# Attention output by token tiles, LN2 statistics in seven operations, part of x + attention on GpSimd, first FFN tiles in blocks of 128

## The reference

```python
x = x + attn(layernorm(x), Wq, Wk, Wv)
x = x + ffn(layernorm(x), W_r, W_k, W_v, mu_r, mu_k)

def attn(x, Wq, Wk, Wv):            # one head of D = 64
    q, k, v = x @ Wq, x @ Wk, x @ Wv
    att = softmax(einsum('bid,bkd->bik', q, k), axis=1)   # over the queries i
    return tile(att @ v, (1, 1, 16))                      # 64 columns, 16 times

def ffn(x, W_r, W_k, W_v, mu_r, mu_k):
    x_prev = x shifted by one token (zeros first)
    xr = mu_r * x + (1 - mu_r) * x_prev
    xk = mu_k * x + (1 - mu_k) * x_prev
    r = sigmoid(xr @ W_r.T)
    return r * (square(relu(xk @ W_k.T)) @ W_v.T)
```

## Time and profile before

| | |
|---|---|
| median of three runs | 393.59 us (393.56 to 395.23) |
| profiled execution | 392.12 us, its span 390.6 us (core 5; cores 386.8 to 390.6) |
| TensorE busy | 313.1 us, 80% |
| ScalarE busy | 229.5 us, 59% |
| VectorE busy | 217.9 us, 56% |
| GpSimd busy | 109.0 us, 28% |
| chain that ended last | PE 48%, ACT 20%, issue 14%, DVE 10%, DMA 4%, POOL 2% |

### The profile page before, as it was taken

How to read it: one execution, slowest core, us unless ns; L and a number is a source line. 1 busy time by engine, 2 the same in 40 slices (tenths; PEclk the granted TensorE clock), 3 DMA queues, 4 the chain that set the end, 5 groups by cost and what they waited for, 6 DMA issues and landing times.

```text
span 390.6 us, 5546 instructions; the slowest of 8 cores (386.8 to 390.6 us)
## 1 busy us (share of the span) xinstructions
PE 313.1 (80%) x1578; PEld 127.5 (33%) x1578; DVE 217.9 (56%) x445; ACT 229.5 (59%) x358; POOL 109.0 (28%) x158
## 2 busy tenths in 40 slices
PE   0467986696869866777536998999999999999993
PEld 0333341231222211111114443444444444444441
DVE  3787889246235321121259987789277918780055
ACT  1442389989799999999849339104840285024500
POOL 2887448608400026888800021001000000000000
PEclk9998897876698986555555899999999999999998
DMA  7999369896899999920000004131423122220014
GB/s 207 297 323 295 109 149 200 165 265 121 117 181 164 178 188 332 343 90 0 1 1 2 0 3 86 28 157 53 79 32 148 68 54 55 107 107 2 0 55 163
DMA packets 40399, 48.10 MB, mean 123 GB/s; under 512 B 31152, under 2 KB 31536, under 8 KB 39984
## 3 DMA queue, kind: packets, MB, share of 16 engines
q1 hardware_dynamic: 39504, 40.98, 37.7%
q0 software_dynamic: 864, 6.75, 10.6%
HBM read 38.74 MB, written 8.39 MB: 121 GB/s over the span
## 4 chain that ended last, share of the span: by engine, by line
PE 48%; ACT 20%; issue 14%; DVE 10%; DMA 4%; POOL 2%; DVEq 0%; ACTq 0%; SPq 0%; POOLq 0%
PE F L1045 13%; PE F L1005 11%; PE F L1023 11%; PE tf L797 5%; ACT junk L1115 5%; ACT junkL L1115 4%; PE F L856 4%; ACT Prot L1115 4%; DMA xst<-x_in 4%; ACT P L1115 3%; DVE xr L646 2%; PE acc L868 2%; ACT z L1143 2%; DVE dxk L655 1%; DVE bnst L458 1%
## 5 line engine op out<-in xcount | busy, mean ns | idle before, releaser
L856 PE MATMUL F<-qk 64*128 64x512 bf16 x136 | 62.0, 476 | 32.1 <-ACT Prot L1115 9.1
L1164 ACT ACTIVATE rr<-F 128x1024 bf16<-128x1024 f32 x16 | 16.4, 1023 | 72.9 <-PE F L1005 72.9
L1005 PE MATMUL F<-wr,xr 128*128 128x512 bf16 x256 | 58.4, 388 | 0.0
L860 PE MATMUL F<-qk 64*128 64x512 bf16 x120 | 57.6, 498 | 0.0
L1045 PE MATMUL F<-wv,ka 128*128 128x512 bf16 x256 | 56.1, 379 | 1.9 <-ACT ka L1172 1.9
L1023 PE MATMUL F<-dxk,wk 128*128 128x512 bf16 x256 | 55.9, 379 | 0.0
L1115 ACT ACTIVATE P<-F,negm 128x1024 bf16<-128x1024 f32 (+1 forms) x40 | 37.2, 947 | 18.5 <-PE F L856 16.3
L1115 ACT ACTIVATE junk<-F,negm 128x1024 bf16<-128x1024 f32 x32 | 39.9, 1260 | 3.0 <-PE F L856 1.7
L856 PEld LDWEIGHTS F<-qk 64*128 64x128 bf16 x136 | 12.5, 97 | 84.1 <-issue 83.0
L1115 ACT ACTIVATE junkL<-F,negm 128x1024 bf16<-128x1024 f32 x32 | 39.9, 1282 | 0.0
L1115 ACT ACTIVATE Prot<-F,negm 128x1024 bf16<-128x1024 f32 x32 | 39.0, 1354 | 0.0
(11 more groups left out here) (105 smaller groups left out, 426.0 us busy)
## 6 DMA issues: line engine op xcount, KB each, us to landing
xst<-x_in SPq DMA_DIRECT2D x32, 512.0 KB, 7.3
x<-x_in SPq DMA_DIRECT2D x16, 512.0 KB, 28.6
y_out<-x SPq DMA_DIRECT2D x15, 512.0 KB, 2.8
wr<-wr_in POOLq DMA_DIRECT2D x1, 2048.0 KB, 15.1
wk<-wk_in POOLq DMA_DIRECT2D x1, 2048.0 KB, 29.3
wv<-wv_in POOLq DMA_DIRECT2D x1, 2048.0 KB, 42.6
y_out<-x SPq DMA_DIRECT2D x2, 256.0 KB, 2.9
wqk<-wqk_in POOLq DMA_DIRECT2D x1, 256.0 KB, 9.3
```

Of the source, the lines that this page charges most:

```text
L856: t.matmul(f[:, 0:512], qk2[0:64, kt * 128:(kt + 1) * 128], qk1[0:64, i0:i0 + 512], start=True, stop=True, skip_group_check=True, tile_pos ...
L860: t.matmul(f[:, 512:1024], qk1[64:128, kt * 128:(kt + 1) * 128], qk2[64:128, i0 + 512:i0 + 1024], start=True, stop=True, skip_group_check= ...
L1005: ins = t.matmul(f[:, hh * 512:(hh + 1) * 512], xr[:, ct, j * 128:(j + 1) * 128], wr[:, ct, hh * 512:(hh + 1) * 512], start=(ct == 0), sto ...
```

## The change

- `out_mm(kt)` has the exponentials of 128 tokens as weights and vs (64 columns) as the moving operand: 16 products of 64 columns, in the order of `LN2OUT`, into acc laid out by token tile. The output is by token at once; the copies of acc, the fp32 transposes and their semaphores are gone. ScalarE copies acc to out_tok in three pieces: tiles 3 to 7, 0 to 2, 8 to 15. The table load for the root stands before the wait for the products.
- out_mm stands behind every second unit only, tiles from 16 on first (`out_after`): 0 to 8 behind units 68 to 84, 16 to 19 to unit 92, then 9 (94), 20 (96), 10 (98) and so on, 15 at unit 118, 29 at 132, 30 and 31 last. x tiles are loaded when theirs is done.
- The loads of wk and wv2 stand behind the folds of tiles 4 and 8.
- `ln2_stats` has seven operations; the first group waits for eight folds only, and comes before any x + attention on VectorE.
- GpSimd adds the attention output to the x tiles of positions 1, 3 and 4 of LN2SEQ (tiles 4, 6, 7), from the first A_TOK on. VectorE adds to positions 0 and 2 behind the group's statistics.
- TensorE turns three z tiles (positions 1, 0, 2), the first two into other PSUM banks, and VectorE evacuates these two. Positions 3 and 4 go by DMA transposes.
- Block 0 is mixed in four blocks of 128 tokens, not two of 128 and one of 256. R(0, 0) and the first half of K(0, 0) wait for each column tile by itself.
- The halo's products stand right behind the last out_mm; its copy before the first x + attention; its two small operations (hx) behind mix_k(0), before the second group's statistics.

```diff
+LN2OUT = [3, 4, 5, 6, 7, 0, 1, 2] + list(range(8, 16))
...
+    for u in range(NB, NU):
+        ready = [k for k in range(KT) if k not in out_pos and last_unit[k] + 4 <= u]
+        if ready and (u - NB) % 2 == 0:
+            kt = min([k for k in ready if k >= 16], default=ready[0])
+            out_after[u] = kt
+            out_pos[kt] = len(out_pos)
...
             def out_mm(kt):
                 t.wait_ge(V_VS, 3 * kt + 3)
-                for w in (0, 2, 1, 3):
-                    half = w // 2
-                    t.matmul(acc[64 * half:64 * half + 64, (w % 2) * 512:(w % 2 + 1) * 512],
-                             vs[:, kt * D:(kt + 1) * D],
-                             own_p(kt)[:, w * 512:(w + 1) * 512],
-                             start=(kt == 0), stop=(kt == KT - 1), skip_group_check=True,
-                             tile_position=(0, 64 * half)).then_inc(P_O, 1)
+                for i, t_ in enumerate(LN2OUT):
+                    ins = t.matmul(acc[:, t_, :], own_p(kt)[:, t_ * 128:(t_ + 1) * 128],
+                                   vs[:, kt * D:(kt + 1) * D],
+                                   start=(kt == out_seq[0] and i % 8 == 0), stop=(kt == KT - 1),
+                                   skip_group_check=True)
+                    if i == 15 or kt == KT - 1 and i == 7:
+                        ins.then_inc(P_O, 1)
...
+            g.wait_ge(A_TOK, 1)
+            for s in GX1:
+                t_ = LN2SEQ[s]
+                g.wait_ge(G_XF, 4 * t_ + 4)
+                g.tensor_tensor(
+                    x1[:, t_, :], x1[:, t_, :],
+                    bass.AP(out_tok, t_ * D, [[TOWN * D, 128], [0, 16], [1, D]]),
+                    ALU.add).then_inc(G_X1, 1)
...
                 v.reduce_sum(so[:, a:b], o, axis=AX.X).then_inc(V_ST2, 1)
...
+                v.scalar_tensor_tensor(w, xf[:, a:b, :], 0.125, o,
                                        ALU.mult, ALU.add).then_inc(V_ST2, 1)
                 v.wait_ge(V_ST2, n + 1)
+                v.scalar_tensor_tensor(od, bass.AP(so, a, [[TOWN, 128], [1, b - a], [0, D]]),
+                                       -1.0 / D, o, ALU.mult, ALU.add).then_inc(V_ST2, 1)
                 v.wait_ge(V_ST2, n + 3)
+                v.tensor_tensor(w, w, od, ALU.mult).then_inc(V_ST2, 1)
                 v.wait_ge(V_ST2, n + 4)
                 v.reduce_sum(sp[:, a:b], w, axis=AX.X).then_inc(V_ST2, 1)
                 v.wait_ge(V_ST2, n + 5)
+                v.scalar_tensor_tensor(vpe2[:, a:b], sp[:, a:b], 1.0 / D, vpe[:, a:b],
                                        ALU.mult, ALU.add).then_inc(V_ST2, 1)
+                v.scalar_tensor_tensor(nmean2[:, a:b], so[:, a:b], -1.0 / D, ag[:, a:b, 0],
+                                       ALU.mult, ALU.subtract).then_inc(V_ST2, 1)
...
             v.wait_ge(A_TOK, 1)
-            ln2_x1(0)
-            v.wait_ge(A_TOK, 2)
-            v.wait_ge(G_XF, 4 * TOWN)
+            v.wait_ge(G_XF, 4 * 8)
             ln2_stats(0)
             ln2_shift(0)
-            for s in range(1, 5):
-                ln2_x1(s)
-            v.wait_ge(D_C, 64)
-            v.wait_ge(A_T2, 2)
+            v.wait_ge(P_H, 2)
+            v.tensor_copy(hs[:, 7:8], F[0][:, 0:1]).then_inc(V_H, 1)
+            ln2_x1(0)
+            ln2_x1(2)
+            v.wait_ge(P_T2, 1)
+            v.tensor_copy(z1T[:, :, c_blk(0):c_blk(0) + 128], tx[1][:, :, :]).then_inc(V_T2, 1)
+            v.wait_ge(P_T2, 2)
+            v.tensor_copy(z1T[:, :, c_blk(0) - 1:c_blk(0)],
+                          tx[0][:, :, 127:128]).then_inc(V_T2, 1)
...
-            mix_d(c_blk(0) + 256, 256, 256, 0, 3)
-            mix_r(c_blk(0) + 256, 256, 256, 0)
+            v.wait_ge(D_T2[1], t2_n(3))
+            mix_d(c_blk(0) + 256, 128, 256, 0, 3)
+            mix_r(c_blk(0) + 256, 128, 256, 0)
+            v.wait_ge(D_T2[0], t2_n(4))
+            mix_d(c_blk(0) + 384, 128, 384, 0, 4)
+            mix_r(c_blk(0) + 384, 128, 384, 0)
```

More of the change, by code:

```diff
@@ L104, in build_program @@
     f_prev = [max([p for p in range(u) if f_of[p] == f_of[u]], default=-1) for u in range(NU)]
+    out_after = {}
+    out_pos = {}
+    for u in range(NB, NU):
[4 more added lines that the diff above has]
+            out_pos[kt] = len(out_pos)
+    for kt in range(KT):
+        if kt not in out_pos:
+            out_pos[kt] = len(out_pos)
+    out_seq = sorted(out_pos, key=out_pos.get)
     ctx = ExitStack()
@@ L300, in build_program @@
         x1_n = lambda q, j: 2 + 4 * q + j
-        NP2 = 5
+        NP2 = 3
+        GX1 = {1: 1, 3: 2, 4: 3}
+        vx1_n = lambda s: s + 1 - sum(p < s for p in GX1)
         t2_n = lambda s: 16 * ((s - NP2) // 2 + 1)
@@ L340, in _ @@
             for t_ in range(TOWN):
-                sy.wait_ge(P_O, 4 * (t_ + 1))
+                sy.wait_ge(P_O, out_pos[t_] + 1)
                 sy.dma_start(out=x1[:, t_, :],
                              in_=x_in[t_ * 128:(t_ + 1) * 128, :]).then_inc(D_R[t_], 16)
+            for s in range(NP2, 5):
+                c0 = 16 + 128 * (LN2SEQ[s] % 8)
+                sy.wait_ge(A_Z1, s + 1)
+                sy.dma_start_transpose(out=z1T[:, :, c0:c0 + 128],
+                                       in_=z1[:, s % 2, :]).then_inc(D_T2[s % 2], 16)
             for q in range(4):
@@ L698, in _ @@
                 if q == 0:
+                    v.wait_ge(V_H, 1)
+                    v.tensor_scalar(hx[:, 0:8], xh[:, :], hs[:, 7:8], None,
+                                    ALU.add).then_inc(V_H, 1)
+                    v.wait_ge(V_H, 2)
+                    v.tensor_tensor(hx[:, 8:16], hx[:, 0:8], hx[:, 0:8],
+                                    ALU.mult).then_inc(V_H, 1)
+                    v.wait_ge(A_TOK, 3)
+                    v.wait_ge(G_XF, 4 * TOWN)
                     ln2_stats(1)
@@ L956, in _, with T2 @@
             VT(3)
-            nxt = begun
-            done = 0
+            assert begun == NB
             t.wait_ge(V_MX, 8)
             t.wait_ge(V_VT, 4)
[L962 to L967, removed]
-            for kt in range(done, KT):
+            for u_ in range(NB, NU):
+                fill(u_)
+                if u_ in out_after:
+                    out_mm(out_after[u_])
+            for kt in out_seq[len(out_after):]:
                 out_mm(kt)
             t.wait_ge(A_EXP, NU)
-            t.wait_ge(D_C, 64)
-            for j in range(8):
-                if j == 0:
-                    t.wait_ge(A_OT, 1)
-                if j == 4:
-                    t.wait_ge(V_OT, 1)
-                ins = t.transpose(F[0][:, j * 128:(j + 1) * 128],
-                                  outT[:, j * 128:(j + 1) * 128], identf[:, :])
-                if j % 4 == 3:
-                    ins.then_inc(P_OTT, 1)
-            def T2(s):
-                if s >= 2:
-                    t.wait_ge(A_T2, s - 1)
-                t.wait_ge(A_Z1, s + 1)
+            for kt in range(KT):
+                for h in range(2):
+                    ins = t.matmul(F[0][64 * h:64 * h + 64, 0:1],
+                                   vs[:, kt * D:(kt + 1) * D],
+                                   junkL[:, halo_unit[kt] % 3, 1054 - kt:1055 - kt],
+                                   start=(kt == 0), stop=(kt == KT - 1),
+                                   skip_group_check=True,
+                                   tile_position=(0, 64 * h))
+                    if kt == KT - 1:
+                        ins.then_inc(P_H, 1)
+            def T2(s, n, to):
+                t.wait_ge(A_Z1, n)
                 for ct in range(CT):
@@ L1003, in R @@
                 for ct in range(CT):
+                    if q == 0 and j == 0:
+                        t.wait_ge(V_XR, ct + 1)
                     for hh in range(2):
@@ L1051, in V @@
                         ins.then_inc(P_F, 1)
-            for s in range(NP2):
-                T2(s)
+            T2(1, 1, tx[1])
+            T2(0, 2, tx[0])
+            t.wait_ge(A_TOK, 3)
+            T2(2, 3, tb[0])
             R(0, 0)
```

159 lines of the change are left out of this document (57 added, 102 removed).

## The result

The changed kernel takes 396.78 us (median of four runs, 396.37 to 396.89) against 393.62 of the kernel before (393.56 to 395.23): ratio 1.0069, 95% interval 1.0042 to 1.0095. It is slower by 3.2 us (0.7%); 395.3 was predicted, from 389.2 to 398.0. Measured again on another chip, beside the experiments, it was 396.78 against 393.88, ratio 1.0073 (1.0052 to 1.0095).

What follows compares the result with a forecast made beforehand. Bound: a serial chain of about 50 us between ScalarE-bound attention and gapless TensorE. Terms -4.20 +5.83 -0.75 +1.15 +0.53 +0.21 -1.11 = +1.66 on 393.59 gave 395.3 us; range 389.2 to 398.0.

Steps and rivals of the forecast that it cites:

- Held adds: LN2 statistics of group 0: GpSimd's three adds and VectorE's two-input operations hold each other for whole instructions, +5.83 us.
- the walk: Statistics to square root, step by step: GpSimd adds alternating with w, od and product, 8.63 us against 2.80.
- The first rival: GpSimd's adds and VectorE's statistics run side by side, nothing held: -4.15, 389.4 us; chance 0.20.
- brief holding: Rival at the statistics: GpSimd's adds hold VectorE, but take near 1.2 us instead of 2.35: 391.8 us; chance 0.13.
- The clock's fall: Rival at V(0, 0): TensorE's clock falls after a gap of about 4 us, +1.9, 397.2; 4 in 10 within each case.
- The likeliest case: Whole kernel: held adds without a fall of the clock, 395.3 us, itself 394 to 396.5; chance 0.37.
- V(0, 0) piece: First V product to R(1, 0): halo products moved to where TensorE waits, -1.11 us; +0.8 if the clock falls.
- Products of 64 columns: Attention output by token tiles: 16 products of 64 columns, 55 ns each at 1.2 GHz, hidden, cost 0.
- The slow end of the range: Attention: products too slow at 1.2 GHz, exponentials starve for units 94 to 118: +3, 398 us; chance 0.05.
- The end of attention: Last vs to LN2 statistics: folding ends near 180, vs takes 0.24, fp32 transposes and copies gone: -4.20 us.
- Statistics no shorter: LN2 statistics of group 0: fewer instructions but no shorter path to the square root, 2.82 against 2.80 us: 0.
- blocks of 128: Mix of block 0: four blocks of 128 take 11.68 us against 10.53: +1.15.

Runs made afterwards that it cites:

- e1: Changed kernel with GpSimd's three x + attention adds given to VectorE, behind the statistics: 394.02 us, ratio 0.9998 to the kernel before.
- e3: Changed kernel with only position 1 added by GpSimd, positions 3 and 4 by VectorE: 394.57 us, ratio 1.0035 to the kernel before.
- e4: Changed kernel with GpSimd filling tiles 4, 6 and 7 with a constant, their adds left out: 391.79 us, ratio 0.9965 to the kernel before.
- e6: Changed kernel with GpSimd's three adds started only after the statistics (after nmr2): 394.64 us, ratio 1.0057 to the kernel before.
- e5: Changed kernel with 12 unused products of 512 columns filling the gap before the first V product: 394.42 us, ratio 1.0026 to the kernel before.
- e7: Changed kernel, GpSimd's adds kept, block 0's last 256 tokens mixed in one block, hx operations moved back, z of position 4 earlier: 393.24 us, ratio 1.0002.
- e8: e2 with the 12 filling products of e5 before the first V product: 390.10 us, ratio 0.9917 to the kernel before.
- e2: e1 with e7's three edits: 392.28 us, ratio 0.9949 to the kernel before.

## Why the prediction came out as it did

**Held adds, the forecast's mechanism: shown.** It was argued from a GpSimd power behind a VectorE add and from a one-input operation of VectorE; e1, e3 and e4 show the missing case, a two-input operation behind a GpSimd add. The term was +5.83 and is +5.63. w took 1.97 where about 2.3 was written, GpSimd's add 2.36 where 2.35 was; the handing to and fro was the walk's: w, add 2, od, add 3, product, their ends 2.55 us apart. The row that the walk rested on, four VectorE adds in 4.63 us around the power, didn't show it, as no add was late there; the second add of e6 does (4.50 for two). The rule in the Trainium skill ("SBUF — State Buffer", Who interferes with whom), that a VectorE instruction with two SBUF inputs contends with a GpSimd one that reads SBUF and not with one that only writes, agrees with this case in both halves: 1.97, 2.62 and 2.44 us beside adds, 0.48 beside a memset (e4). The first rival, 389.4, and brief holding fall.

**The clock's fall: in the rivals with 4 in 10, and it happened.** The likeliest case had left it out, and this is why 395.3 was too low; the same case with the fall was 397.2, and 396.8 was measured. The step of the sum that was mis-sized is the V(0, 0) piece: -1.11 written, +0.36 measured, 1.47 of it the clock (15.57 less the 14.10 that 15.21 - 1.11 gives). The price set, 1.9, was a little high: e5 puts it at 1.6. The gap was forecast at 4 us, and is 2.85: K's products after mix_k ran at 0.55 of the clock from 229.4 to 233, and the gap covered this slowness. Just before, the pieces of K(0, 0) had come one by one, 0.67 us apart with 0.29 idle, each when mix_k had its column tile. That alone isn't the reason for this first fall, though: e6 has the same pauses, its clock stays at 1.00 there, and its gap is 3.75. What else it takes is open, and so is the forecast's rule that the gap's length decides, as e7 shows. The changed kernel, then e6:

```profile
225.00:229.40 4.40, 2.65 (x8) 0.57 (x7) 4.40 (x8) 1.02 (x1) 0.00 (x0) 0.98 0.00 0
229.40:233.00 3.60, 3.57 (x10) 1.31 (x11) 3.28 (x7) 0.00 (x0) 0.00 (x0) 0.55 0.00 0
```
```profile
223.40:227.80 4.40, 2.77 (x11) 0.72 (x9) 4.38 (x8) 1.02 (x1) 0.00 (x0) 1.00 0.00 0
227.80:231.40 3.60, 3.60 (x17) 1.65 (x18) 3.30 (x6) 0.00 (x0) 0.00 (x0) 1.00 0.02 5
```

**Products of 64 columns: right.** 16 take 1.01 us at 1.2 GHz, the last of them 0.24, so 51 ns apart; the other out_mm at this clock have 53 (55 written). First out_mm to last vs is unchanged. The slow end of the range and the rule of the Trainium skill ("TensorE: Matmul & The Clock Gate", Part 3) that a load overlaps only a product of other row groups would have shown as starved exponentials; the measurement decides against them. The clock kept higher for longer in attention, as argued (0.77 in 150 to 165, 0.50 before the change), and was worth nothing there.

**The end of attention: right to 0.2 us, one reason wrong.** The last vs takes 0.24 and statistics start 2.04 behind it. But folding did not end near 180. x tile 9 was asked for at 148.86 and landed at 167.86; the nine tiles before it had taken 3.2 to 5.4 us each. While it was under way, wk (140.12 to 158.29) and wv2 (from 153.47) were loading and the DMA engines were busy throughout (share 1.03 from 154 to 168). So the weights probably stood in its way, against what the forecast says of them, but no run moved them. Core 0's last fold ended at 192.86, 3.7 us before the vs: the 0.24 had less room than was written.

```profile
153.47 0.57 POOL L454 DMA_DIRECT2D wv<-wv_in  x1
...
168.01 1.25 POOL L439 TENSOR_TENSOR fold<-x 128x512 f32<-128x512 f32 x1 [13.97 <-DMA x<-x_in]
```
```profile
154.00:168.00 14.00, 10.87 (x125) 5.90 (x126) 1.69 (x9) 14.00 (x28) 0.04 (x1) 0.75 1.03 196
```

**Statistics no shorter, blocks of 128, hx, statistics 1, halo: right.** The statistics of group 0 took 2.83 us in e1 against 2.80 before and 2.82 written; blocks and hx 1.81 against 1.68; statistics 1 0.16 against 0.21. The halo's -1.11 is seen where the clock is kept: 13.95 from V(0, 0) to R(1, 0) in e5 against 15.21, -1.26. R(0, 0) began 1.3 us after the first mix and gave nothing.

**Not in the sum.** R(1, 0) to the end is 0.78 shorter. TensorE's part is the same in both (110.50 us from R(1, 0) to V(3, 0)), so it lies in the tail behind it: from the end of VectorE's last add to the end of the span, where the last store runs, it is 3.5 us before and 2.65 after in the mean of the cores. And the time rose 0.7 us more than the pieces (3.16 against 2.47), which may be due to the core that happened to be late before the first out_mm. Both were seen, not tested, and the forecast had neither. They nearly cancel, so that 397.2 for the case with the fall comes within 0.4 us of the time is in part luck; the agreement piece by piece is not.

## What to carry to other kernels

Before giving GpSimd a share of VectorE's work, count the SBUF inputs of what VectorE does meanwhile: an operation with two on VectorE and one of GpSimd that reads (here adds, folds and powers) take turns, whole instruction by whole instruction, and a long GpSimd add in front of a chain of short VectorE steps charges every step. Here an add of 1.14 us on VectorE was cheaper than one of 2.35 on GpSimd beside it. When a serial chain ahead of a dense product stream grows, look at TensorE's gap too: its clock can turn a covered wait into a cost behind it, here 1.6 us.

## What the runs showed of the hardware

- Holding works both ways and is handed over at every instruction, also between two that follow each other on one engine: three GpSimd adds alternated with three VectorE operations (7.43 us for what takes 7.1 alone). It applies to fp32 and bf16 alike (the mix of e6, 2.08 against 0.70) and not to a reduction with one input (0.49) or a GpSimd memset (three in 2.73 us). One input doesn't always exempt VectorE: the bf16 scaling of vs took 1.05 and 0.68 us beside GpSimd folds, and 0.24 without.
- A gap of 2.85 us before V(0, 0) let the granted clock fall from 1.00 to 0.50 (2.73 to 2.96 on the cores of two measurements, all of which show it); 1.68 to 2.23 before had not, nor did 1.17 in e8. One of 3.75 let it fall on every core in e2 and not on six cores of e7.
- Filling the gap with products whose result nobody reads kept it at 1.00 and gave back 1.6 us.
- GpSimd adds 128x1024 fp32 in 2.35 us, VectorE in 1.22; products of 64 columns, each with a load of 128, start 53 ns apart at 1.2 GHz and 30 at 2.4 GHz, where 64 columns alone are 53 and 27 ns.
